# Slot release and tile stores of three edge passes: who waits, who issues

## The reference

```python
x = _layernorm(x + _L0_gnn_ref(x, edge_index, ...))        # attention over in-edges, softmax per node, 8 heads
x = _layernorm(x + _L1_gnn_ref(x, edge_index, ...))        # two graph convolutions:
    # h = x @ W1; out = segment_sum(h[src] * norm, dst) + b; layer_norm; relu; the same with W2
x = _layernorm(x + _L2_gnn_ref(x, edge_weight, ...))       # hw = h @ W
    # agg = segment_sum(hw[src] * sym_norm[:, None], dst); relu(agg + b)
x = _layernorm(x + _L3_gnn_ref(x, edge_index, ...))        # direction-mixed messages, softmax weights, 4 heads
```

## Time and profile before

| | us |
|---|---|
| median of 3 runs | 6573.53 (6570.21 to 6581.08) |
| profiled execution, first to last instruction | 5313.9 |
| layer 0, up to pass 1's first gather | 1236 |
| passes 1, 2, 3 | 1007, 1007, 993 |
| mix stage and end | 1071 |

### The profile page before, as it was taken

The page is one execution under the profiler, slowest core; times in us unless marked ns, Lnnn a source line. Parts: engine busy times, 40 slices in busy tenths (PEclk is TensorE's granted clock), DMA queues, the critical chain, the costliest instruction groups (busy, mean ns, idle before and its releaser), DMA issues.

```text
span 5313.9 us, 86764 instructions
## 1 busy us (share of the span) xinstructions
PE 3931.6 (74%) x13357; PEld 2389.2 (45%) x13357; DVE 3517.2 (66%) x10780; ACT 2554.6 (48%) x6938; POOL 3875.0 (73%) x3995
## 2 busy tenths in 40 slices
PE   6888888887777777677777777777677656666763
PEld 4666666664444444344444443343333333444442
DVE  6789888885554545444444445666666578888887
ACT  1667667664555555455545552000000166666665
POOL 3777777775777777677777776777777677777775
PEclk8889889988899998887777777877888777777776
DMA  5444444443333333443333333333333322222222
GB/s 151 113 122 126 122 126 124 120 121 98 111 112 112 111 112 111 118 139 111 111 112 112 111 112 100 109 109 109 109 108 109 98 57 57 57 57 57 57 57 68
DMA packets 252628, 549.14 MB, mean 103 GB/s; under 512 B 71467, under 2 KB 136235, under 8 KB 252108
## 3 DMA queue, kind: packets, MB, share of 16 engines
q0 software_dynamic: 178752, 478.34, 32.8%
q1 hardware_dynamic: 66972, 58.64, 3.5%
q10 hardware_dynamic: 6384, 6.62, 0.5%
HBM read 501.16 MB, written 42.15 MB: 102 GB/s over the span
## 4 chain that ended last, share of the span: by engine, by line
PE 32%; POOL 22%; DMA 18%; issue 13%; DVE 6%; ACT 6%; SPq 2%; DVEq 1%; ACTq 0%; POOLq 0%
PE bank L1453 18%; POOL scratch L1863 12%; DMA scratch<-tab_x,src_idx 10%; POOL scratch L1399 9%; DMA scratch<-tab_h,src_idx 7%; PE bank L1297 4%; PE bank L172 4%; PE bank L1154 3%; DVE reg_acc L1463 2%; ACT scratch L1066 2%; POOL reg_x L1024 2%; SPq L865 1%; DVE reg_acc L1322 1%; PE bank L1142 1%; PE bank L157 1%
## 5 line engine op out<-in xcount | busy, mean ns | idle before, releaser
L1453 PE MATMUL bank<-scratch 128*128 x4986 | 1946.5, 501 | 739.9 <-SPq L1414 356.6
L1463 DVE TENSOR_TENSOR reg_acc<-reg_acc,bank 128x256 f32 x2493 | 1047.3, 420 | 1368.2 <-PE bank L1453 1310.3
L1399 POOL DMA_INDIRECT scratch<-tab_x,src_idx x1566 | 1494.3, 954 | 533.5 <-issue 259.4
L1453 PEld LDWEIGHTS bank<-scratch 128*128 128x128 f32 x4986 | 961.2, 229 | 1630.2 <-issue 1582.6
L1024 POOL DMA_INDIRECT reg_x<-tab_h,src_idx x832 | 838.7, 1008 | 302.7 <-issue 184.1
L1399 POOL DMA_INDIRECT scratch<-tab_h,src_idx x783 | 746.6, 953 | 264.7 <-issue 153.0
L1863 POOL DMA_INDIRECT scratch<-tab_h,src_idx x783 | 743.0, 949 | 249.3 <-issue 226.8
L1916 PE MATMUL bank<-reg_w,scratch 128*128 128x260 f32 x1664 | 639.8, 527 | 282.7 <-issue 180.1
L1423 ACT ACTIVATE scratch<-iota_row,dst_loc 128x128 f32<-128x128 f32 x1662 | 579.6, 393 | 345.5 <-PE bank L1453 336.1
L1297 PE MATMUL bank<-reg_x,scratch 128*128 128x265 f32 x1664 | 582.4, 461 | 72.7 <-DVE reg_x L1339 70.4
L1916 PEld LDWEIGHTS bank<-reg_w,scratch 128*128 128x128 f32 x1664 | 376.3, 252 | 505.1 <-issue 305.0
(11 more groups left out here) (313 smaller groups left out, 4364.1 us busy)
## 6 DMA issues: line engine op xcount, KB each, us to landing
scratch<-tab_x,src_idx POOLq DMA_INDIRECT x1566, 2.8
scratch<-tab_h,src_idx POOLq DMA_INDIRECT x1566, 2.7
reg_x<-tab_h,src_idx POOLq DMA_INDIRECT x832
tab_h<-scratch ACTq DMA_DIRECT2D x7, 924.0 KB, 5.2
reg_x<-in_x SPq DMA_DIRECT2D x7, 896.0 KB, 11.3
reg_w<-in_x SPq DMA_DIRECT2D x49, 128.0 KB, 2.3
tab_x<-reg_acc SPq DMA_DIRECT2D x49, 128.0 KB
tab_xs<-reg_w SPq DMA_DIRECT2D x49, 128.0 KB, 2.6
```

Source lines behind the costliest of these rows:

```text
L1399: e.indirect_dma_start(ring_rows[:, j % SLOTS, :], None, self.table, bass.IndirectOffsetOnAxis(ap=src_idx[:, j:j + 1], axis=0)).then_inc(* ...
L1453: e.matmul(self.bank(i), ring_hots[:, i % HOTS, :], rows, start=True, stop=True).then_inc(*self.product.up)
L1463: e.tensor_tensor(v, v, self.bank(i), ALU.add).then_inc(*self.added.up)
```

## The change

In passes 1 to 3 SP frees the slots as it does in the mix stage, and POOL waits for that (`free(j - 60)`). SP's list no longer holds the stores; ScalarE issues each right behind its copy, after a wait for that copy. The products of each pass get a semaphore of their own, so that SP can wait for a count from the table. The words of the tables are packed with the count in the low 10 bits (before: the count above bit 16), and both the steps' counts and SP's are masked before they are waited for, in the mix stage too.

```diff
-AHEAD = SLOTS - (NODE_TILES - 1)
-PLACES = 2 ** 16
+PLACE_BITS = 10
+PLACES = 2 ** PLACE_BITS
-STORE_AT = [min(WHOLE[k] + PARTS + 3 - k, POSITIONS) for k in range(T)]
@@ slot_rows, chunks_needed, steps_through
-            e.reg_alu(parts[0], words[t % GROUP], PLACES - 1, op=ALU.bitwise_and)
+            e.reg_alu(parts[0], words[t % GROUP], PLACE_BITS, op=ALU.logical_shift_right)
-            e.reg_alu(parts[1], words[t % GROUP], 16, op=ALU.logical_shift_right)
+            e.reg_alu(parts[1], words[t % GROUP], PLACES - 1, op=ALU.bitwise_and)
-            return e.snap(end_regs[c % ENDS_AT_ONCE], min_val=1, max_val=STEPS)
+            e.reg_alu(end_regs[ENDS_AT_ONCE], end_regs[c % ENDS_AT_ONCE], PLACES - 1, op=ALU.bitwise_and)
+            return e.snap(end_regs[ENDS_AT_ONCE], min_val=1, max_val=STEPS)
@@ class EdgePass
             def gpsimd(self, e):
                 for j in range(POSITIONS):
-                    if j >= AHEAD:
-                        e.wait_ge(*self.product(j - AHEAD))
+                    if j >= SLOTS:
+                        e.wait_ge(*self.free(j - SLOTS))
-            def sync(self, e, table, taken, stored, at):
-                done = 0
-                for j in range(POSITIONS + 1):
-                    while done < T and STORE_AT[done] == j:
-                        e.wait_ge(*taken(done))
-                        e.dma_start(node_rows(table, done, done + 1), at(done)).then_inc(*stored[done % len(stored)].up)
-                        done += 1
-                    if j < POSITIONS:
-                        e.wait_ge(*self.got[j % ARRIVALS](j // ARRIVALS))
-                        e.sem_inc(*self.landed_n.up)
+            def sync(self, e):
+                for j in range(POSITIONS):
+                    c = j - SLOTS + FREE_EARLY
+                    if inside(c, POSITIONS - SLOTS):
+                        if c % ENDS_AT_ONCE == 0:
+                            load_ends(e, c, min(ENDS_AT_ONCE, POSITIONS - SLOTS - c))
+                        e.wait_ge(self.product.sem, steps_through(e, c))
+                        e.sem_inc(*self.free.up)
+                    e.wait_ge(*self.got[j % ARRIVALS](j // ARRIVALS))
+                    e.sem_inc(*self.landed_n.up)
@@ pass1_scalar (pass2_scalar and pass3_scalar alike, with taken_l2, taken_l3 and their tables)
                         e.mul(sums[:, k, :], dense2.out(k), dinv[:, k:k + 1]).then_inc(*taken2.up)
+                        e.wait_ge(*taken2(k))
+                        e.dma_start(node_rows(tab_h2, k, k + 1), acc[:, k:k + 1, 0:FEAT]).then_inc(*h2_stored.up)
```

More of the change, by code:

```diff
@@ L330, in build @@
         s_landed = [signal(f"pass{k}_landed") for k in (1, 2, 3, 4)]
+        s_through = [signal(f"pass{k}_product") for k in (1, 2, 3)]
         s_free = signal("slot_free")
@@ L740, in ranks @@
                                        op1=ALU.add).then_inc(*pre_v.done("slot_of"))
-                e.tensor_scalar(landed_of, position, 1.0, float(PLACES), ALU.add,
-                                ALU.mult).then_inc(*pre_v.done("landed_of"))
+                e.tensor_scalar(landed_of, position, 1.0, None, ALU.add).then_inc(*pre_v.done("landed_of"))
                 e.wait_ge(*pre_v.at("landed_of"))
-                e.scalar_tensor_tensor(out=slot_i, in0=slot_of, scalar=float(FEAT), in1=landed_of, op0=ALU.mult,
+                e.scalar_tensor_tensor(out=slot_i, in0=slot_of, scalar=float(FEAT * PLACES), in1=landed_of, op0=ALU.mult,
                                        op1=ALU.add).then_inc(*pre_v.done("slot_i"))
@@ L863, in load_ends @@
             if not end_regs:
-                end_regs.extend(e.alloc_register(f"end{k}") for k in range(ENDS_AT_ONCE))
+                end_regs.extend(e.alloc_register(f"end{k}") for k in range(ENDS_AT_ONCE + 1))
             e.load(end_regs[0:n], ends_row[0:1, c0:c0 + n])
         def steps_through(e, c):
-            return e.snap(end_regs[c % ENDS_AT_ONCE], min_val=1, max_val=STEPS)
+            e.reg_alu(end_regs[ENDS_AT_ONCE], end_regs[c % ENDS_AT_ONCE], PLACES - 1, op=ALU.bitwise_and)
+            return e.snap(end_regs[ENDS_AT_ONCE], min_val=1, max_val=STEPS)
         def rank_value(e, name, t):
@@ L1377, in build, with __init__ @@
         class EdgePass:
-            def __init__(self, table, weighted, landed, banks):
+            def __init__(self, table, weighted, landed, product, banks):
                 self.table, self.weighted, self.banks = table, weighted, banks
@@ L1388, in __init__ @@
                 self.got = [s_slot[k].take(len(range(k, POSITIONS, ARRIVALS))) for k in range(ARRIVALS)]
-                self.product, self.added = s_edge.take(RANKED), s_added.take(RANKED)
+                self.product, self.added = product.take(RANKED), s_added.take(RANKED)
+                self.free = s_free.take(POSITIONS - SLOTS)
+                assert self.product.base == 0
                 if weighted:
@@ L1444, in step @@
                     load_slots(e, "tensor", i)
-                rows, needed = slot_rows(e, "tensor", i, 0, FEAT), chunks_needed(e, "tensor", i)
+                needed = chunks_needed(e, "tensor", i)
+                rows = slot_rows(e, "tensor", i, 0, FEAT)
                 if self.weighted:
@@ L1670, in pass2_scalar @@
                         e.copy(staged[:, k % 2, :], dense_l2.out(k)).then_inc(*taken_l2.up)
+                        e.wait_ge(*taken_l2(k))
+                        e.dma_start(node_rows(tab_x2, k, k + 1),
+                                    staged[:, k % 2:k % 2 + 1, :]).then_inc(*x2_stored[k % 2].up)
         def pass2_vector(e):
@@ L1747, in pass3_sync @@
         def pass3_sync(e):
-            edges3.sync(e, tab_h3, taken_l3, h3_stored, lambda k: staged[:, k % 2:k % 2 + 1, 0:ROW3])
+            edges3.sync(e)
         def pass3_tensor(e):
@@ L1783, in pass3_scalar @@
                         e.copy(staged[:, k % 2, 0:ROW3], dense_l3.out(k)).then_inc(*taken_l3.up)
+                        e.wait_ge(*taken_l3(k))
+                        e.dma_start(node_rows(tab_h3, k, k + 1),
+                                    staged[:, k % 2:k % 2 + 1, 0:ROW3]).then_inc(*h3_stored[k % 2].up)
         def pass3_vector(e):
@@ L1941, in turn_about @@
                     load_slots(e, "scalar", i)
-                row, needed = slot_rows(e, "scalar", i, SIDE3, ROW3), chunks_needed(e, "scalar", i)
+                needed = chunks_needed(e, "scalar", i)
+                row = slot_rows(e, "scalar", i, SIDE3, ROW3)
                 e.wait_ge(s_landed[3].sem, needed)
```

10 lines of the change are left out of this document (5 added, 5 removed).

## The result

The changed kernel takes 6520.6 us (median of 6 runs, 6500.2 to 6524.4); the kernel before, beside it, 6570.8 (6 runs, 6553.8 to 6581.1). The ratio is 0.9924 (95% interval 0.9901 to 0.9947), so the change makes the kernel 50 us faster, where 7 us had been predicted and 6540 to 6592 us given as the range.

What follows compares the result with a forecast made beforehand. It took POOL's issuing of gathers to bound passes 1 to 3. Its terms, -7.0 and +0.15, summed to -6.9 us: 5307.0 for the profiled execution, carried to the runs as 6567 us, range 6540 to 6592.

Steps and rivals of the forecast that it cites:

- The 1260 us: Whole kernel: runs' median 1259.6 us above the profiled span, read as a constant outside it or as slower TensorE.
- The second reading: All stages: in the runs TensorE is at its lower clock, 1.2 GHz, which gives 6560 us in all.
- Masks: 0: TensorE's steps and SP: TensorE keeps its instructions and SP's mask falls in idle time, so 0 us.
- POOL's hole, -7.0: Start of pass 2: POOL's 7.31 us wait on TensorE shrinks to the usual 0.30, -7.0 us.
- +0.05 us a pass for the store: Tails of the passes: ScalarE issues the store in 0.37 instead of 0.32 us, +0.15 us in all.
- The lead through SP: Passes 1 to 3: SP's frees, raised only after arrival j - 9, come in time for POOL; cost 0.
- SP's reads: Passes 1 to 3: 52 table reads a pass, 1.62 us each, hidden; cost 0, bounds 0 and +253 us.
- SP without stores: SP's waits for ScalarE in the passes: their going is worth 0, bounds 0 and -10 us in all.
- R4: SP's place in its list limits POOL's lead to nine, not 60; +94 us, 6668 us, chance 0.03.
- R2: Passes 1 to 3: longer lead carries TensorE over slow stretches; one pass gains 30 us, 6543 us, chance 0.25.
- R3: Pass 1: SP's reads hold back landings and starve TensorE; 42 us in one pass, 6609 us, chance 0.17.
- R1: Nothing gained: the lower-clock reading holds or TensorE takes back pass 2's hole; 6573 us, chance 0.17.

Runs made afterwards that it cites:

- e3_masks: The kernel before with only the table words packed anew and the counts masked, on a long chip: 6521.2 us, ratio 0.9926.
- y1: The changed kernel run once more, on another long chip, against the kernel before: 6573.0 us, ratio 0.9912.
- y3: The changed kernel with a redundant mask on VectorE's slot word in the mix stage, on a long chip: 6613.7 us, 0.9967 of the kernel before.
- x1: e3_masks with a redundant mask on VectorE's slot word in the mix stage, on a short chip: 5309.7 us, 1.0000 of the kernel before.
- x2: e3_masks with SP's mask in the mix stage done twice, on a short chip: 5313.1 us, 1.0007 of the kernel before.
- z1: The changed kernel with two more masks on VectorE's slot word in the mix stage, on a short chip: 5306.0 us, 0.9995 of the kernel before.
- y2: The kernel of x1 (masks alone, VectorE's redundant mask given back) on a long chip: 6628.9 us, 0.9986 of the kernel before.
- x3_after_dve_op: The changed kernel with a redundant mask on VectorE's slot word in the mix stage, on a short chip: 5307.2 us, 1.0001 of the kernel before.
- third set: Runs on another long chip of the changed kernel and variants against the kernel before, which took 6634.7 us; the changed kernel took 6573.0 us.
- first set: Runs on a long chip of the change taken apart, against the kernel before at 6562.5 us; the masks alone took 6521.2 us.

## Why the prediction was wrong

**The 1260 us, the first step that failed.** The prediction saw that the span was 1259.6 us under the runs and took it for a constant, or for TensorE at its lower clock. Neither holds. Wherever the record has a timed run's own span, it is within 2 us of its time; the profiled execution was simply not an execution of the length that the runs had. The Trainium skill (Runtime: NRT & Kernel Launch, "The ~15µs preamble/postamble breakdown") puts what surrounds a kernel at some 9 to 15 us; here the runs' times leave 2 us for it. Layer 0, which the change does not touch, is 294 us longer in the changed kernel's trace. The second reading, TensorE at 1.2 GHz throughout, asks for a clock near 0.5 where the long runs have 0.72 to 0.74. Its 6560 us fitted the median by chance. The prediction's last sentence, that the 1260 us may hide what decides, was the right warning, yet the chances gave a faster kernel 0.27.

**"Masks: 0", the term that failed.** Measured on long chips it is -41 us: e3_masks against before, and again y1 against y3, which is 41 of the changed kernel's 62 us there. The prediction looked at TensorE, whose step keeps its count of instructions, and at SP, which gets one more; it did not look at VectorE, where a mask and a copy become one fused shift, 832 times in the mix stage. For the traced execution 0 was right (x1, x2, z1: nothing). For the runs it was not, and by the traced execution alone it could not be seen: there VectorE waits 83 us for ScalarE ahead of the very instruction that uses the word (the row of x1_dve_op above), which hides the record. Of the other 21 us on that chip 15 lie between y2 and y3, which differ by frees and stores, and 6 between y2 and before, which the interval of y2 (up to 1.0001) doesn't tell from none.

**POOL's hole, -7.0.** Right in the place and size where it was worked out: 7.31 became 0.30 us, pass 2 lost 8 us. But the kernel as a whole gained only 1.3 to 4.6 us on short chips (the seven sets with the change, each with small register work added or altered; the changed kernel itself was not run on one). Pass 1 gave back some 2 us of it: its gathers take 1.9 us more in all, for which the prediction had no term, and at its end POOL waits 20.85 us for the table, where x1_dve_op has 20.32 and the kernel before 19.32. ScalarE's store is issued at 2242.11, at the moment at which SP, no longer held by the copy, begins to issue pass 2's loads; before, the store went first. That the two collide was not tested. The term "+0.05 us a pass for the store" is thus too small for pass 1, where the tail grew by 0.5 to 1.5 us. On long chips the hole is there too (7.69 us in y2_dve_op, 0.31 in y3_after_dve_op), but it is one of hundreds of waits of POOL.

**The lead through SP, SP's reads, SP without stores.** On short chips 0, as said: POOL's waits for SP never pass the usual 0.3 us in x3_after_dve_op, and pass 1 keeps its clock (0.92 in x1 and in x3), so the reads did not lower it. On long chips POOL waits 698 us for SP's frees, which is R4's picture, yet without its price: the kernel is not slower. Frees and stores together are worth 15 us there in the third set (y3 against y2); by the ratios of the first comparison and the first set, 0.9924 against the masks' 0.9926, they are worth nothing; with the stores left on SP the frees cost 69 us. The stores' place is thus what keeps the frees free of charge, which the prediction had at -10 to 0 for SP and saw no tie to the frees.

**The rivals.** R2 had the sign and a price of 30 us (6543), but for the larger part not the cause: e3_masks has the old lead and a gain of 41 us. What may be R2's is the 15 us of y3 against y2, with pass 2 shorter; that the lead brings them was not tested apart from the stores. R3's price (42 us in one pass) did not come, though pass 1 is 8 to 25 us longer with the frees. On short chips the whole kernel is level with before, which is R1's number (x3_after_dve_op 1.0001, 0.9990 to 1.0012), but not its reasons: the hole in pass 2 was closed.

## What to carry to other kernels

If the profiled span and the timed runs differ by more than a few microseconds, the profile is of another kind of execution: first get a trace whose span is that of the runs, and see how long a stage is there that the change leaves alone; put no small term at zero because its cover shows in the other trace. Count records on every engine, also where the source line looks like a swap of one operation for another, and count them apart from their times. Where one engine's list both frees buffers and waits for late work (a tile's store), take the two apart together.

## What the runs showed of the hardware

The same program takes 5309 us on four chips and 6562 or 6635 us on two others, with TensorE's matmuls busy 3909 us on the one kind and 4229 on the other, its weight loads 2379 and 2708, and the other engines alike. On the long ones the medians of the register records stay (40 and 122 ns on VectorE), but a few records stall for some 0.70 us: 495 of TensorE's 8311 and 191 of SP's 1648 last over 0.5 us in y2_dve_op, none in x1_dve_op. The idle time without a releaser ahead of VectorE's L2022 goes from 12 to 173 us. There 832 masks of 0.04 us are worth 41 us, while 0.086 us a step in longer records at the same count cost nothing (y2_dve_op against before, 0.9986). On the short chips two masks more a step (z1_dve_two_ops) or a record of 0.12 us made 0.04 (z4_plain_words) are worth nothing. What stalls the records, and what makes a chip long, is not shown by any row here.
